# A gated cross- and self-attention block: high parts of queries and keys copied on the chip, and a new order of TensorE's work in the self stage

## The chip, the cores and the metric

The kernel runs on one core of a Trainium2 chip. The metric is the device time of one execution in microseconds (us). Three runs of the kernel before took 2587.09 to 2594.41 us, median 2592.28. All times in timelines are us from the start of the profiled execution's span.

## What is computed

Inputs are x of 32 batches x 100 rows x 512, and a context of 32 x 722 x 512. There are 16 heads of 32. The part that matters here is the second half:

```python
x = x + tanh(g_xattn) * cross_attention(layernorm(x), ctx)
h = layernorm(x)
qkv = (h @ W_qkv).reshape(B, N, 3, 16, 32)
sim = mean over heads of cos(q[:, 5:], q_g)      # scaled to 0..1 over all batches
pos = sim > 0.9
# masked_attn(m): softmax(q k^T / sqrt(32) over the 5 registers and the tokens with m) @ v
x_pos, x_neg = masked_attn(pos), masked_attn(~pos)
reg_out = (x_pos[:, :5] + x_neg[:, :5]) * 0.5
tok_out = where(pos, x_pos[:, 5:], x_neg[:, 5:])
x = x + tanh(g_ffn) * (concat(reg_out, tok_out) @ W_proj + b_proj)
```

All of it is to be exact to about fp32. Fast matmuls take inputs rounded to a short format (fp32r in the listings), so a factor is split into a high and a low part, and a product is three products: high x high, high x low and low x high.

## The kernel before

Four stages follow each other: queries of the cross attention, cross attention, rows (output of the cross attention, layernorm, the q, k and v of the self attention), and the self stage, `stage_self`, from about 2249 us to the end. The rows stage leaves the high and low parts of q and k in DRAM in `qk_parts` (parts 0 to 3: q high, q low, k high, k low), transposed, and values, x1 and the mask tables beside them.

The self stage takes the 32 batches one by one. Its queries and keys come in pairs of batches: `load_pair` fills `q_stack[buf]` and `k_stack[buf]`, each [98, 16 heads, two batches], where rows 0 to 95 are three places of 32 rows each: q high, q low, q high, against k high, k high, k low. One matmul over the 98 rows so gives all three products and, by the last two rows, the mask. A third of either stack is therefore a second copy of a high part, and `load_stacks` (L928) loads it from DRAM as well: for q one load of 64 rows and one of 32, for k one of 32 and one of 64, in pieces of 800 bytes (two batches of one row and head), 1024 pieces for 64 rows and 512 for 32. `load_tables` (L936) adds four small loads of 32 pieces. There are three such buffers (STACKS), so pair p+3 is loaded when pair p has been scored.

All engines run the same loop over batches, written out six batches long (RING), and they meet through semaphores. In `body(b)`, the scores and the softmax of batch b+1, the transposition and mixing of batch b and the projection of batch b-1 stand together:

- SP (queue of loads and stores, in order): store y of b-1 (waits `y_ready`), load x1, wait for `mix_full` of b, load the values of b+3, and in even b load the pair of b+6. Pair 3 follows the mixing of batch 0 in this order, pair 4 that of batch 2.
- PE: `turn_probs(b, n)` transposes a quarter of the probabilities (four heads) into `turned[n % 2]` (L1834), `score(b + 1, j)` makes a quarter of the scores (L1827), `mix(b, n)` multiplies by the values (L1845), `project(b - 1, half)` the output projection (L89 to L91). The order is turn 0, score 0, turn 1, score 1, turn 2, score 2, mix 0, mix 1, project first half, turn 3, score 3, project second half, mix 2, mix 3.
- DVE: `turn_back` n copies a transposed quarter to `pt` (L1750), `shift_of` takes the minimum of the (negated) scores (L1739), `fold_registers` (L1762, L1764), `split_mix` makes `ot_lo` (L1768), `invert` the reciprocals (L1746), `result` makes y (L1775). Order: copy 0, minimum 0, fold, copy 1, split, minimum 1, copy 2, minimum 2, reciprocal 0, copy 3, minimum 3, reciprocal 1, result, reciprocals 2 and 3. There are two y buffers; `result` waits until the store of two batches before has landed.
- ACT: `high_part` makes `ot_hi` of b-1 (L1705), then exponentials 0 to 3 of b+1 (L1713).
- POOL: scales the four quarters of the probabilities (L1679), each after its reciprocal; in even b it then waits for the loads of pair b/2+1 and copies its register columns (L951).

## Time and profile before

| what | value |
|---|---|
| median of three runs | 2592.28 us |
| profiled execution: time, span | 2588.93, 2587.1 us |
| PE busy in the span | 2478.7 us, 96% |
| DVE, ACT, POOL busy | 1804.8, 1332.2, 491.6 us |
| mean granted TensorE clock | 0.971 |
| queue q1 (SP's loads and stores) | 375.71 MB, 61.2% of 16 engines' span |

The self stage is the last 13% of the span. In the page's forty slices it is the last five or so: DMA is at nine tenths there and TensorE's clock at eight or nine tenths. A timeline shows each instruction's start and duration; for SP the duration is that of the issue, not of the transfer. TensorE's matmuls are pipelined, so a duration is longer than the distance to the next start.

### The profile page before, as it was taken

How to read it: one execution, taken by the hardware profiler on the slowest of the kernel's cores; microseconds unless marked ns; L12 is line 12 of the kernel's file. 1: busy time of each engine (PE TensorE's matmuls, PEld its weight loads, DVE VectorE, ACT ScalarE, POOL GpSimd, SP SyncE). 2: the span in 40 equal slices, each digit the busy share in tenths (PEclk: the TensorE clock that was granted, in tenths of full speed). 3: DMA queues.
4: the chain of work that ended last, by engine and by line, in shares of the span. 5: the costliest groups of instructions: out<-in, count | busy, mean ns of one | idle time of the engine just before them, and what ended most of it. 6: DMA issues, size and time to landing. Idle time of an engine off the chain costs nothing. (4 is left out here: it accounts for less than half of the span.)

```text
span 2587.1 us, 47522 instructions
## 1 busy us (share of the span) xinstructions
PE 2478.7 (96%) x17128; PEld 2223.4 (86%) x17128; DVE 1804.8 (70%) x2998; ACT 1332.2 (51%) x3000; POOL 491.6 (19%) x412
## 2 busy tenths in 40 slices
PE   6899999999999999999999999999959999889998
PEld 6889999999999999999999999999858888677776
DVE  7567777777777777777777777777757666565665
ACT  3355555555555545555555555545534444455564
POOL 0311111111111111111111111111024333133333
PEclk9999999999999999999999999999969999889999
DMA  7645554555545555545554455554459999899994
GB/s 223 205 122 131 124 131 120 131 128 131 132 117 128 130 133 128 131 117 130 129 132 122 128 125 129 131 132 126 106 150 192 214 211 198 207 175 189 192 185 105
DMA packets 324312, 379.82 MB, mean 147 GB/s; under 512 B 125814, under 2 KB 231702, under 8 KB 324118
## 3 DMA queue, kind: packets, MB, share of 16 engines
q1 hardware_dynamic: 322414, 375.71, 61.2%
q8 instruction: 132, 2.16, 0.4%
q10 hardware_dynamic: 1704, 1.43, 0.2%
q14 instruction: 62, 0.51, 0.1%
HBM read 162.48 MB, written 72.57 MB: 91 GB/s over the span
## 5 line engine op out<-in xcount | busy, mean ns | idle before, releaser
L740 DVE TENSOR_TENSOR c_parted<-c_prob,c_parted 128x600 fp32r<-128x600 f32 x512 | 400.6, 783 | 363.4 <-ACT c_prob L686 363.4
L864 PE MATMUL c_mix<-c_parted,c_v 120*66 120x200 f32 (+1 forms) x3072 | 544.9, 270 | 0.7 <-DVE c_parted L740 0.6
L849 PEld LDWEIGHTS c_pair<-c_q_stack,c_k_stack 100*120 100x120 f32 (+1 forms) x3072 | 517.7, 186 | 10.7 <-issue 6.1
L849 PE MATMUL c_pair<-c_q_stack,c_k_stack 100*120 100x100 f32 (+1 forms) x3072 | 520.0, 227 | 6.1 <-DVE c_parted L740 4.5
L726 DVE TENSOR_REDUCE c_peak<-c_pair 100x1 f32<-100x724 f32 x512 | 456.9, 908 | 55.2 <-PE c_pair L811 39.7
L682 ACT ACTIVATE c_parted<-c_pair 128x600 fp32r<-128x600 f32 x512 | 344.9, 674 | 283.0 <-PE c_pair L849 282.8
L864 PEld LDWEIGHTS c_mix<-c_parted,c_v 120*66 120x66 f32 (+1 forms) x3072 | 418.3, 140 | 3.1 <-DVE c_parted L740 0.9
L664 ACT ACTIVATE c_v<-c_work 120x512 fp32r<-120x512 f32 (+1 forms) x192 | 115.7, 603 | 442.3 <-PE c_work L91 442.3
L686 ACT ACTIVATE c_prob<-c_pair 128x600 f32<-128x600 f32 x512 | 341.4, 667 | 0.0
L811 PE MATMUL c_pair<-c_k_stack,c_q_stack 96*100 96x362 f32 x1024 | 254.4, 329 | 0.0
L617 POOL TENSOR_TENSOR c_ct_lo<-e_stage,c_ct_hi 128x722 fp32r<-128x722 f32 x64 | 111.8, 1747 | 747.1 <-ACT c_ct_hi L650 747.1
L617 POOL TENSOR_TENSOR f_ct_lo<-e_stage,f_ct_hi 128x722 fp32r<-128x722 f32 x60 | 104.8, 1747 | 718.5 <-ACT f_ct_hi L650 718.5
L811 PEld LDWEIGHTS c_pair<-c_k_stack,c_q_stack 96*100 96x100 f32 x1024 | 169.6, 166 | 60.4
L674 ACT ACTIVATE c_k_hi<-c_work,f_key_bias 128x362 fp32r<-128x362 f32 (+1 forms) x256 | 144.9, 567 | 105.3 <-PE c_work L91 85.7
L720 DVE SCALAR_TENSOR_TENSOR c_k_lo<-c_work,f_key_bias,c_k_hi 128x362 fp32r<-128x362 f32 (+1 forms) x256 | 149.8, 586 | 54.4 <-ACT c_k_hi L674 54.4
L1713 ACT ACTIVATE s_prob<-s_scores,s_shift 106x100 f32<-106x100 f32 x512 | 168.1, 368 | 34.5 <-DVE s_shift L1739 34.5
L89 PE MATMUL c_work<-f_ct_hi,w_wk_hi 128*128 128x362 f32 (+1 forms) x512 | 176.7, 345 | 8.6 <-PEq L153 4.5
L89 PE MATMUL c_work<-c_ct_hi,w_wk_hi 128*128 128x362 f32 (+1 forms) x512 | 175.0, 342 | 0.0
L91 PE MATMUL c_work<-f_ct_hi,w_wk_lo 128*128 128x362 f32 (+1 forms) x512 | 169.4, 331 | 0.0
L90 PE MATMUL c_work<-f_ct_lo,w_wk_hi 128*128 128x362 f32 (+1 forms) x512 | 169.1, 330 | 0.0
L91 PE MATMUL c_work<-c_ct_hi,w_wk_lo 128*128 128x362 f32 (+1 forms) x512 | 167.9, 328 | 0.0
L90 PE MATMUL c_work<-c_ct_lo,w_wk_hi 128*128 128x362 f32 (+1 forms) x512 | 167.9, 328 | 0.0
(205 smaller groups left out, 5292.7 us busy)
## 6 DMA issues: line engine op xcount, KB each, us to landing
c_k_stack<-c_k_hi SPq DMA_DIRECT2D x1024, 90.2 KB, 2.1
e_stage<-in_ctx SPq DMA_DIRECT2D x32, 1444.0 KB, 6.3
c_k_stack<-c_k_lo SPq DMA_DIRECT2D x512, 90.2 KB, 2.1
c_q_stack<-q_parts SPq DMA_DIRECT2D x192, 100.0 KB, 2.4
mix_parts<-w_mixed SPq DMA_DIRECT2D x64, 200.0 KB, 3.2
r_parts<-mix_parts SPq DMA_DIRECT2D x22, 512.0 KB, 7.1
s_q_stack<-qk_parts SPq DMA_DIRECT2D x10, 800.0 KB
s_k_stack<-qk_parts SPq DMA_DIRECT2D x10, 800.0 KB
```

Source lines behind the costliest of these rows:

```text
L89: pe.matmul(out, left_hi, right_hi, start=first, stop=False)
L90: pe.matmul(out, left_hi, right_lo, start=False, stop=False)
L91: return pe.matmul(out, left_lo, right_hi, start=False, stop=last)
L617: pool.tensor_tensor(ct_lo[odd][:, k, :], columns[:, k, :], ct_hi[odd][:, k, :], ALU.subtract).then_inc(ct_lo_done, 1)
L682: act.activation(parted[i % PR][:, :, 0, :].rearrange("p (a t) s -> p a t s", a=2), logits, ACT.Exp).then_inc(exp_hi_done, 1)
L686: act.activation(prob[i % 2][:, :, :].rearrange("p (a t) s -> p a t s", a=2), logits, ACT.Exp).then_inc(exp_done, 1)
L726: dve.tensor_reduce(peak[:, i:i + 1], pair[i % 2][0:S, :, 0:HALF], AX.XY, ALU.max).then_inc(peak_done, 1)
L740: dve.tensor_tensor(p[:, :, 1, :], prob[i % 2][:], p[:, :, 0, :], ALU.subtract).then_inc(p_lo_done, 1)
L811: last = pe.matmul(pair[i % 2][0:S, bank, 0:HALF], q_stack[0:STACK, i, :], k_stack[0:STACK, i, cols], start=True, stop=True)
L849: return pe.matmul(pair[i % 2][0:r, t // (CT // 2), col:col + S], k_stack[:, i, c_cols(t)], q_stack[:, i, :], start=True, stop=True)
L864: return pe.matmul(mix[g % 2][0:VW, at * 2 * S:(at + 1) * 2 * S], v[0:r, t, i, :], parted[i % PR][0:r, t, :, :].rearrange("p a s -> p (a s)"),
L1713: last = act.activation(prob[:, j, k, :], scores[0:QR, j, k * S:(k + 1) * S], ACT.Exp, bias=shift[:, at:at + 1], scale=-1.0, accum_out=tot ...
```

## The change

From pair 3 on, `load_stacks` makes one load for q (places 0 and 1) and one for k (places 1 and 2). The missing third is copied on the chip, in four pieces of four heads: ACT copies q high from place 0 to place 2, DVE copies k high from place 1 to place 0. The pieces of pair p stand in the bodies of batches 2p-4 (pieces 0 and 1) and 2p-3 (2 and 3); the first scores of the pair are made in the body of 2p-1. A piece waits for the pair's loads. In ACT's order a piece stands behind exponentials 1 and another behind exponentials 3; in DVE's order one behind reciprocal 0, ahead of copy 3, and one behind reciprocal 1, ahead of the result. POOL's register copies wait for q's third, the first score of a pair for both. Pairs 0 to 2 are loaded whole, in a changed order of k's two loads.

TensorE's order becomes turn 0, score 0, turn 1, score 1, turn 2, score 2, turn 3, score 3, the whole projection of b-1, then mix 0 to 3. Turn 3 gets a wait for DVE's copy 1, and the wait for `y_ready` stands ahead of the mixing, now behind the projection.

```diff
-A_PAIR_LOADS = 8
+WHOLE_LOADS, PAIR_LOADS = 8, 6
+WHOLE_PAIRS = 3
+
+
+def pair_landed(buf, before):
+
+    return 16 * (PAIR_LOADS * (before + 1) + (WHOLE_LOADS - PAIR_LOADS if buf < WHOLE_PAIRS else 0))
...
-def load_stacks(engine, qk_parts, q_stack, k_stack, first, landed):
-    for stack, at, places in ((q_stack, SIDE, ((0, 0, 2), (2, 0, 1))), (k_stack, 0, ((0, 2, 1), (1, 2, 2)))):
-        for place, part, parts in places:
+def load_stacks(engine, qk_parts, q_stack, k_stack, first, landed, whole=True):
+    for stack, at, places in ((q_stack, SIDE, ((0, 0, 2), (2, 0, 1))), (k_stack, 0, ((1, 2, 2), (0, 2, 1)))):
+        for place, part, parts in places if whole else places[:1]:
             src = qk_parts[part:part + parts].rearrange("a (d h) n -> (a d) h n", h=H)
             engine.dma_start(f32(stack[place * HD:(place + parts) * HD, :, at:at + 2 * S]),
                              src[:, :, bass.ds(first * S, 2 * S)]).then_inc(landed, 16)
...
+        def thirds_in(i, before, more):
+
+            ahead = (i + 4 - i % 2) // 2
+            if not more or (before < RING and ahead < WHOLE_PAIRS):
+                return 0, 0, ()
+            return ahead % STACKS, ahead // STACKS, (2, 3) if i % 2 else (0, 1)
...
                 pool.memset(f32(q_stack[buf][0:STACK, :, at:at + 1]), 0.0).then_inc(cleared, 1)
             pool.wait_ge(cleared, 2 * (STACKS - 1))
 
-            def copies(buf, pairs_before):
-                pool.wait_ge(pair_in[buf], (pairs_before + 1) * 16 * A_PAIR_LOADS)
+            def copies(buf, pairs_before, whole=False):
+                pool.wait_ge(pair_in[buf], pair_landed(buf, pairs_before))
+                if whole is not True:
+                    pool.wait_ge(q_third, HPT * (STACKS * pairs_before + buf - WHOLE_PAIRS + 1))
                 copy_registers(pool, q_stack[buf], unit_column, copies_done)
...
-            def body(b, i, deep, pair, before, last):
+            def copy_third(buf, before, n):
+                act.wait_ge(pair_in[buf], pair_landed(buf, before))
+                heads = slice(n * HPT, (n + 1) * HPT)
+                act.activation(q_stack[buf][2 * HD:3 * HD, heads, SIDE:SIDE + 2 * S],
+                               f32(q_stack[buf][0:HD, heads, SIDE:SIDE + 2 * S]), ACT.Copy).then_inc(q_third, 1)
+
+            def body(b, i, deep, pair, before, last, u, more=True):
                 odd = i % 2
                 if before:
                     high_part(b - 1, 1 - odd)
+                buf, turns, pieces = thirds_in(i, before, more)
+                half = len(pieces) // 2
                 if not last:
-                    for j in range(HPT):
-                        exponentials(b + 1, 1 - odd, j)
+                    exponentials(b + 1, 1 - odd, 0)
+                    exponentials(b + 1, 1 - odd, 1)
+                for n in pieces[:half]:
+                    copy_third(buf, u + turns, n)
+                if not last:
+                    exponentials(b + 1, 1 - odd, 2)
+                    exponentials(b + 1, 1 - odd, 3)
+                for n in pieces[half:]:
+                    copy_third(buf, u + turns, n)
...
-            def body(b, i, deep, pair, before, last):
+            def copy_third(buf, before, n):
+                dve.wait_ge(pair_in[buf], pair_landed(buf, before))
+                heads = slice(n * HPT, (n + 1) * HPT)
+                dve.tensor_copy(k_stack[buf][0:HD, heads, 0:2 * S], f32(k_stack[buf][HD:2 * HD, heads, 0:2 * S])
+                                ).then_inc(k_third, 1)
...
+                buf, turns, pieces = thirds_in(i, before, more)
+                half = len(pieces) // 2
                 turn_back(b, 0)
                 if not last:
                     shift_of(b + 1, 0)
                 if not last:
                     shift_of(b + 1, 2)
                     invert(b + 1, 1 - odd, 0)
+                for n in pieces[:half]:
+                    copy_third(buf, u + turns, n)
                 turn_back(b, 3)
                 if not last:
                     shift_of(b + 1, 3)
                     invert(b + 1, 1 - odd, 1)
+                for n in pieces[half:]:
+                    copy_third(buf, u + turns, n)
                 if before:
...
-            def score(b, i, j, pairs_before):
+            def score(b, i, j, pairs_before, whole=False):
 
                 buf, odd = i // 2, i % 2
                 if not odd and j == 0:
-                    pe.wait_ge(pair_in[buf], (pairs_before + 1) * 16 * A_PAIR_LOADS)
+                    pe.wait_ge(pair_in[buf], pair_landed(buf, pairs_before))
                     pe.wait_ge(copies_done, 2 * STACKS * pairs_before + 2 * buf + 2)
+                    if not whole:
+                        pe.wait_ge(q_third, HPT * (STACKS * pairs_before + buf - WHOLE_PAIRS + 1))
+                        pe.wait_ge(k_third, HPT * (STACKS * pairs_before + buf - WHOLE_PAIRS + 1))
...
                 turn_probs(b, 2)
                 if not last:
                     score(b + 1, at, 2, step)
-                if before > 1:
-                    pe.wait_ge(y_ready, b - 1)
-                mix(b, odd, 0, place, deep)
-                mix(b, odd, 1, place, deep)
+                pe.wait_ge(pt_done, b * HPT + 2)
+                turn_probs(b, 3)
+                if not last:
+                    score(b + 1, at, 3, step)
                 if before == 1:
                     pe.wait_ge(w_split, 2)
                 if before:
                     project(b - 1, 1 - odd, 0)
-                turn_probs(b, 3)
-                if not last:
-                    score(b + 1, at, 3, step)
-                if before:
                     project(b - 1, 1 - odd, 1)
-                mix(b, odd, 2, place, deep)
-                mix(b, odd, 3, place, deep)
+                if before > 1:
+                    pe.wait_ge(y_ready, b - 1)
+                for n in range(HPT):
+                    mix(b, odd, n, place, deep)
```

## Rows read from the trace of the kernel before

**Rows 1.** Busy time in stretches: engine busy us (instructions), granted clock, DMA share, GB/s.

```profile
2380.00:2400.00 20.00, 17.19 (x142) 13.89 (x141) 11.17 (x31) 10.27 (x60) 6.61 (x10) 0.91 0.94 192
...
2552.68:2561.12 8.44, 8.44 (x78) 6.96 (x77) 6.10 (x16) 5.84 (x33) 3.38 (x5) 1.00 0.24 76
```

**Rows 2.** Timeline of SyncE's queue: start, duration of the issue, line.

```profile
2249.64 1.29 SPq L932 DMA_DIRECT2D s_q_stack<-qk_parts  x2
...
2262.71 3.04 SPq L932 DMA_DIRECT2D s_q_stack<-qk_parts  x2
...
2284.54 3.01 SPq L932 DMA_DIRECT2D p_q_stack<-qk_parts  x2
...
2302.60 2.97 SPq L932 DMA_DIRECT2D s_q_stack<-qk_parts  x2
...
2500.50 3.55 SPq L932 DMA_DIRECT2D s_q_stack<-qk_parts  x2
...
2517.76 0.56 SPq L1635 DMA_DIRECT2D out<-s_y  x1
...
2521.76 3.05 SPq L932 DMA_DIRECT2D p_q_stack<-qk_parts  x2
```

**Rows 3.** DMA of one period, from 2362.19 to 2382.22.

```profile
DMA packets 3918, 3.74 MB, mean 186 GB/s; under 512 B 258, under 2 KB 3330, under 8 KB 3916
```

**Rows 4.** Waits from 2303 to 2540: us, times, longest.

```profile
DVE s_y L1775 <- DMA out<-s_y: 38.1, 12, 5.7
```

**Rows 5.** Timeline of TensorE: start, duration, instruction, [idle before <- released by].

```profile
2552.68 0.57 PE L1834 MATMUL s_turned<-e_ident,s_prob 106*100 106x106 f32 x4
...
2554.94 1.31 PE L1845 MATMUL s_out_bank<-s_pt,s_values 100*32 100x106 f32 x16
...
2556.18 0.47 PE L89 MATMUL s_out_bank<-s_w_hi,s_ot_hi 128*100 128x512 f32 x1
```

**Rows 6.** Timeline of DVE in the same batch.

```profile
2554.58 0.59 DVE L1750 COPY s_pt<-s_turned 100x424 f32<-100x424 f32 x1
...
2555.24 0.57 DVE L1768 TENSOR_TENSOR s_ot_lo<-s_out_bank,s_ot_hi 128x400 fp32r<-128x400 f32 x1
...
2557.20 0.17 DVE L1746 RECIPROCAL s_inv<-s_total 106x4 f32<-106x4 f32 x1
```

**Rows 7.** Timeline of POOL, its register copies at the start of the stage.

```profile
2267.07 0.59 POOL L951 TENSOR_TENSOR s_q_stack<-s_q_stack,p_unit_column 96x80 fp32r<-96x80 f32 x2 [8.18 <-DMA s_q_stack<-tables]
...
2290.23 0.61 POOL L951 TENSOR_TENSOR s_q_stack<-s_q_stack,p_unit_column 96x80 fp32r<-96x80 f32 x2 [4.42 <-DMA s_q_stack<-tables]
```

**Rows 8.** Groups by line and shape, whole span: busy us, mean ns | idle before.

```profile
L1679 POOL TENSOR_TENSOR s_prob<-s_prob,s_inv 106x400 f32<-106x400 f32 x128 | 107.8, 854 | 192.7 <-DVE s_inv L1746 192.5
...
L650 ACT ACTIVATE c_ct_hi<-e_stage 128x722 fp32r<-128x722 f32 x64 | 51.0, 796 | 0.0
...
L1440 DVE COPY w_mixed<-w_mixed 32x224 f32<-32x224 f32 x1 | 0.3, 265 | 0.0
...
L1806 DVE TENSOR_TENSOR s_w_lo<-e_stage,s_w_hi 128x2048 fp32r<-128x2048 f32 x1 | 5.3, 5331 | 1.6 <-ACT s_w_hi L1726 1.6
...
L1304 DVE TENSOR_TENSOR r_w_lo<-e_stage,r_w_hi 128x2048 fp32r<-128x2048 f32 x1 | 2.3, 2292 | 0.8 <-ACT r_w_hi L1197 0.8
```

**Rows 9.** Timeline of TensorE, whole self stage.

```profile
2284.38 0.57 PE L1834 MATMUL s_turned<-e_ident,s_prob 106*100 106x106 f32 x4
...
2307.11 0.92 PE L1834 MATMUL s_turned<-e_ident,s_prob 106*100 106x106 f32 x4 [4.25 <-POOL s_prob L1679]
...
2316.55 0.57 PE L1834 MATMUL s_turned<-e_ident,s_prob 106*100 106x106 f32 x4
...
2407.88 2.10 PE L1845 MATMUL s_out_bank<-s_pt,s_values 100*32 100x106 f32 x16 [0.93 <-DMA s_values<-values]
...
2512.36 0.57 PE L1834 MATMUL s_turned<-e_ident,s_prob 106*100 106x106 f32 x4
...
2569.56 0.93 PE L1834 MATMUL s_turned<-e_ident,s_prob 106*100 106x106 f32 x8
```

More of the change, by code:

```diff
@@ L1593, in stage_self @@
         cleared = m.sem("cleared")
+        q_third, k_third = m.sem("q_third"), m.sem("k_third")
         block = ctx.enter_context(nc.Block())
@@ L1600, in all_batches, with load_pair @@
             for i in range(RING):
-                body(i, i, i // DEEP, i // 2, i, False)
+                body(i, i, i // DEEP, i // 2, i, False, 0)
             with engine.Fori(1, TAIL // RING) as u:
                 for i in range(RING):
-                    body(u * RING + i, i, u * (RING // DEEP) + i // DEEP, u * STACKS + i // 2, RING, False)
+                    body(u * RING + i, i, u * (RING // DEEP) + i // DEEP, u * STACKS + i // 2, RING, False, u)
             for b in range(TAIL, B):
-                body(b, b % RING, b // DEEP, b // 2, RING, b == B - 1)
+                body(b, b % RING, b // DEEP, b // 2, RING, b == B - 1, b // RING, (b + 4 - b % 2) // 2 < PAIRS)
+        def thirds_in(i, before, more):
[3 more added lines that the diff above has]
+            return ahead % STACKS, ahead // STACKS, (2, 3) if i % 2 else (0, 1)
         @block.sync
         def _(sp):
-            def load_pair(first, buf):
-                load_stacks(sp, qk_parts, q_stack[buf], k_stack[buf], first, pair_in[buf])
+            def load_pair(first, buf, whole=False):
+                load_stacks(sp, qk_parts, q_stack[buf], k_stack[buf], first, pair_in[buf], whole)
                 load_tables(sp, table_dram, q_stack[buf], k_stack[buf], first, pair_in[buf])
@@ L1622, in _ @@
             sp.wait_ge(cleared, 2 * (STACKS - 1))
-            load_pair(2, 1)
+            load_pair(2, 1, True)
             load_values(1, 1)
@@ L1630, in _ @@
             for n in range(2, STACKS):
-                load_pair(2 * n, n)
+                load_pair(2 * n, n, True)
             def store(b, odd):
@@ L1686, in _ @@
                 if b % 2 == 0:
-                    copies((b + 2) // 2 % STACKS, (b + 2) // RING)
+                    copies((b + 2) // 2 % STACKS, (b + 2) // RING, (b + 2) // 2 < WHOLE_PAIRS)
             with pool.Fori(1, TAIL // RING) as u:
@@ L1697, in _ @@
                 if b % 2 == 0 and b + 2 < B:
-                    copies((b + 2) // 2 % STACKS, (b + 2) // RING)
+                    copies((b + 2) // 2 % STACKS, (b + 2) // RING, (b + 2) // 2 < WHOLE_PAIRS)
         @block.scalar
@@ L1776, in result, with body @@
                                          ).then_inc(y_ready, 1)
-            def body(b, i, deep, pair, before, last):
+            def copy_third(buf, before, n):
[3 more added lines that the diff above has]
+                                ).then_inc(k_third, 1)
+            def body(b, i, deep, pair, before, last, u, more=True):
                 odd = i % 2
+                buf, turns, pieces = thirds_in(i, before, more)
+                half = len(pieces) // 2
                 turn_back(b, 0)
@@ L1865, in body @@
                 if not last:
-                    score(b + 1, at, 0, step + (i + 1) // RING)
+                    score(b + 1, at, 0, step + (i + 1) // RING, before < RING and (i + 1) // 2 < WHOLE_PAIRS)
                 if before:
@@ L1883, in body @@
                     project(b - 1, 1 - odd, 0)
-                turn_probs(b, 3)
-                if not last:
-                    score(b + 1, at, 3, step)
-                if before:
                     project(b - 1, 1 - odd, 1)
-                mix(b, odd, 2, place, deep)
-                mix(b, odd, 3, place, deep)
+                if before > 1:
+                    pe.wait_ge(y_ready, b - 1)
+                for n in range(HPT):
+                    mix(b, odd, n, place, deep)
             for j in range(HPT):
-                score(0, 0, j, 0)
+                score(0, 0, j, 0, True)
             for i in range(RING):
```

## The prediction

> **What bounds the kernel now.** I read the page first: TensorE is busy 96% of the span, so a share of busy time decides nothing, and the change touches only the self stage, the last 340 us. There I read stretches of 20 us, then the stretch of one batch late in the stage, then the queue of SyncE, then each engine's timeline.
>
> Two regimes stand side by side. In the middle of the stage the DMA engines are busy 94%, TensorE only 17.2 of 20 us, and its granted clock is 0.91 in one such stretch [rows 1]. In the batch from 2552.68 to 2561.12, when no pair loads are left, TensorE is busy in all of its 8.44 us at full clock, while DVE has 6.10, ACT 5.84 and POOL 3.38 us of work and DMA is at 0.24 [rows 1]. So a batch costs 8.44 us when TensorE alone sets it.
>
> The middle does not reach that. SP issues the loads of a pair of batches at 2302.60 for the fifth pair and at 2521.76 for the sixteenth and last: 11 periods in 219.2 us, 19.9 us a pair. Of such a period the issue itself takes 17 us (2500.50 to the store at 2517.76) [rows 2], because the queue is full. One period moves 3918 packets [rows 3]; by the code 3072 of them are the 800-byte pieces of queries and keys, some 600 are values, x1 and results, 128 are tables. The stores wait behind the pair's loads in SP's queue, and so the result on DVE waits for a y buffer, 38.1 us in 12 times in this stretch [rows 4]; behind it wait the reciprocals, POOL's scaling and TensorE's transposition. The reader is to see that the bound of the middle is the DMA traffic seen through one in-order queue, with TensorE 1.4 us a batch behind it.
>
> **What the loads cost after the change.** From the fourth pair on, the third load of q (32 partitions) and of k go: 1024 of 3072 packets. Priced from three places: the steady period, 19.9 us for 3800/16 = 237 packets an engine, 84 ns each; the first pair of the stage, issued at 2249.64 and landed when POOL's copies began at 2267.07, 17.4 us [rows 2, 7], at most 17.4/206 = 84 ns (values of one batch with it, and nothing taken off for latency); the second, issued at 2262.71 behind the first and landed by 2290.23, 23.2 us after the first for some 231 packets, 100 ns. So 64 packets fewer an engine are 4.8 to 6.4 us (lower end: pair one with 2 us of latency taken off, 75 ns); I take 84 ns, 5.4 us. The DMA period falls to about 14.5 us, under 2 x 8.44. DMA stops being the rate.
>
> **What the order on TensorE costs.** Work is the same, but two covers go. In the covered batch, counted from its first transposition at 2552.68, three transposition-score pairs take 2.26 us, half of the mixing 1.24 us, then the projection starts at 3.50 [rows 5]. The fourth transposition needs the buffer that copy 1 on DVE frees, done at 2554.58+0.59, so 2.49; the projection needs ot_lo, done at 2555.24+0.57, so 3.13 [rows 6]. Before, mixing lay between, so both were ready. Now the fourth transposition is next at 2.26 and waits until about 2.5, and the projection follows its scores at about 3.25, just after ot_lo. That is 0.3 us of waiting a batch: 8.7 us, 17.4 a pair. In the other direction, scores 3 come 2.7 us earlier, so exponentials 3 have more room.
>
> **What the copies cost.** ACT gets two copies a batch of 32 partitions x 800 elements. Nearest row: a copy in SBUF of 722 elements, 0.80 us [rows 8]; scaled 0.88. 5.84+1.76 = 7.6 us, below 8.7. DVE gets two as well. The nearest row is a copy in SBUF of 224 elements, 0.27 us [rows 8]: between 0.27 (nothing scales) and 0.95 (all scales); I take the middle, 0.6. 6.10+1.2 = 7.3 us, at the upper end 8.0. Neither is the bound by itself. The Trainium skill (VectorE: DVE Perf Modes, "Mode 2x_2P") says an fp32 copy within SBUF runs at two elements a cycle; by its figure for such copies (the section on the TRN2 errata) one would take an estimated 0.48 us and the sum would be the same.
>
> **The added wait.** Both engines now wait for the load itself. DVE's first copy of a pair stands behind reciprocal 0, which is at 2557.20, 4.5 us into the batch [rows 6], so at about 4.7; behind it are queued copy 3 of the probabilities, the minimum of scores 3, the result and the reciprocals 1 to 3. ACT's stands behind exponentials 1 at about 5.1; behind it exponentials 2 and 3. TensorE's transpositions 2 and 3 of the next batch and mixing 3 of this one wait for those. Going through that order, DVE may come 1.2 us late and ACT 1.4 before TensorE is held: DVE by the chain minimum, exponentials 3, reciprocal, scaling.
>
> The load is issued some 0.7 us after the mixing of batch b, an even one, and is wanted in b+2: 8.7+4.7 = 13.4 us after that mixing, harmless until 14.6. When does it land? Pair one with 5.4 us off lands 12.0 us after issue: 12.7. With pair two's 100 ns for 128+8 packets of its own and 19 of store, x1 and values ahead, plus 1 us until the first packet: 16.5, so 17.2. I take the middle, 15.0: 0.4 us late a pair. So 17.8 us a pair (17.4 to 20.0).
>
> POOL's register copies now wait for ACT's thirds, a batch ahead of their use: nothing, as those end within a microsecond of exponentials 3, whose scaling POOL awaits anyway. TensorE's added waits for both are a batch old by then: nothing. SP's stores come out of its queue earlier; nothing waits for that any more.
>
> **The sum**, against the profiled execution (span 2587.1, time 2588.93; the median of the runs is 2592.28, 3.35 above). Start: whole loads of pairs 1 and 2 are as before. Pair 3 is issued at 2284.54 [rows 2] and is now wanted in batch 2, which begins at 2284.38 [rows 9], so at 2289.1, and lands at about 2298: 9 us, less 1.2 of slack, 7.7, and TensorE restarts at a low clock. What that costs is seen in batch 4 before, where after 4.25 us idle a group of transpositions takes 0.92 us rather than 0.57 [rows 9]; the slow stretch there costs about 2.4 us. That stall of batch 4, 6.65 in all, goes. With 0.3 x 3 for the order: +7.7+2.4+0.9-6.65 = +4.4. Middle: from 2316.55 to 2512.36 [rows 9] 10 pairs took 195.8 us, now 178.0: -17.8. End: batches 25 to 30, 57.2 us to 2569.56 [rows 9], now 6 x 8.7: -5.0. The last batch has no scores between its transpositions to cover copy 1 and ot_lo, and loses the cover of mixing for both: an estimated 8.65 us for 7.55, +1.1. Together -17.3 us: 2571.6 for the profiled execution, 2575.0 from the median. I say 2573.
>
> **The rivals.** (a) The load comes late, and the clock makes it dear: slower than before. Price: at 100 ns a packet it lands at 17.2, 2.6 past the slack. The trace shows what idle time of that size does: after 0.93 us without work the mixing of 2407.88 takes 2.10 us where it is 1.31 in a covered batch [rows 5, 9], and with the projection after it some 1.6 us are lost. A pair is then 17.4+2.6+1.6 = 21.6, 2.0 more than now: 10 x 2.0 + 4.4 - 5.0 + 1.1 = +20, so 2612. It is slower from a pair of 19.6, that is, from a landing at about 15.2 if the clock falls with it, or 16.8 if not. Against it: the traffic ahead is lighter than for pair two. (b) DVE and POOL get into each other's way. POOL's scaling starts as soon as reciprocal 0 or 1 ends, exactly when DVE's copies start. The row for it: a subtraction of 2048 elements on DVE takes 2.29 us alone and 5.33 while POOL scales four times [rows 8]. If each copy waits for a scaling of 0.85 us [rows 8], DVE has 7.3+1.7 = 9.0 a batch and its late reciprocals hold transpositions: 9.1 to 9.3 a batch, 18.4 a pair: -11, 2581. The Trainium skill states the rule (SBUF — State Buffer, "Who interferes with whom"): a two-port copy and a GpSimd instruction exclude each other and the first to start keeps the ports; by it, if DVE starts first, POOL waits and nothing is lost. The trace agrees that one is held for long: 5.33 against 2.29 us. (c) The packets are not what fills the queue (a fixed cost a load, the tables), and the period stays near 19.6: the change does not do what it says, within 5 us of before. For it: the issue times show that the queue is full, not what fills it. Against: the stage's DMA share of 0.94 falls to 0.24 as soon as pair loads are over [rows 1]. (d) A pair lands in between, 18.4 to 19.3, near -5 us: the same within what can be told.
>
> **Chances.** Forecast (17.0 to 18.2 a pair) 0.60, 2565 to 2581; (b) 0.11; (a) 0.14; (c) 0.06; (d) 0.09. A measurement of this kernel tells 0.3%, 8 us. Faster: 0.60+0.11 = 0.71; same: 0.15; slower: 0.14. The range from 2563 to 2596 leaves out about 0.06 below and most of (a) above.
>
> **What would show it.** SP's issue of a pair down from 17 to 10 to 12 us with gaps behind it; DMA share of the middle near 0.75; no wait of the result for a store; DVE's and ACT's thirds at 0.6 and 0.9 us; a wait of about 0.25 us before the fourth transposition in each batch; a wait of about 9 us for the load in batch 2, then under 1 us a pair. Wrong if DVE's first third of a pair waits 2 us or more, if the clock in the middle is below 0.95, or if a batch at the end takes over 9 us.

## The result, and the profile after

The changed kernel takes 2585.7 us (median of 11 runs, 2582.55 to 2589.23) against 2592.28 (11 runs of before, 2585.11 to 2596.53): a ratio of 0.9978, 95% interval 0.9970 to 0.9986. That is 5.7 us (the medians lie 6.6 apart), about a third of the forecast of 17.3. The sign was right and the size was not. The time lies in the stated range and near the price of rival (d). The profiled execution has a span of 2585.0 us and a time of 2586.86.

First the stage by stretches. A batch is counted from its first transposition (L1834 before, L1880 after), read from TensorE's timeline; all numbers are us.

| | batch 0 starts | batches 0 to 4 | 5 to 24 (a pair) | 25 to 30 | 31 to the end | span |
|---|---|---|---|---|---|---|
| before | 2255.69 | 60.86 | 195.81 (19.58) | 57.20 | 17.54 | 2587.1 |
| forecast, change | 0 | +4.4 | -17.8 (17.80) | -5.0 | +1.1 | -17.3 |
| after | 2259.03 | 70.43 | 184.87 (18.49) | 54.52 | 16.15 | 2585.0 |
| measured, change | +3.3 | +9.6 | -10.9 | -2.7 | -1.4 | -2.1 |

The later start of batch 0 comes from ahead of the stage, in code that the change doesn't touch (the stage's first load of q and k is issued at 2252.99 for 2249.64), and over the profiles of this study it lies between 2255.7 and 2262.9 us. So single spans are worth less here than the stretches and the ratios of the runs.

The middle first, as in [rows 1]: the same columns, after.

```profile
2380.00:2400.00 20.00, 17.84 (x157) 14.12 (x155) 14.48 (x36) 15.18 (x70) 8.70 (x11) 1.00 0.66 155
...
2544.16:2552.40 8.24, 8.03 (x77) 6.67 (x77) 6.05 (x16) 5.73 (x33) 3.93 (x7) 1.00 0.25 75
```

DMA is no longer the bound: its share is 0.66 where it was 0.94. A covered batch at the end takes 8.24 us; it was 8.44, and the forecast for it was 8.7. Two such batches would be 16.5 us, yet a pair takes 18.49. TensorE is without work 2.16 us in those 20. The waits, from 2330 to 2500, say behind whom (total us, times, longest). The group of [rows 4], the result's wait for a store, is gone, in the stretch of that row too.

```profile
DVE s_k_stack L1812 <- DMA s_q_stack<-tables: 12.7, 6, 2.8
DVE s_inv L1777 <- ACT s_prob L1729: 10.4, 16, 0.9
ACT s_q_stack L1736 <- DMA s_q_stack<-tables: 10.0, 6, 2.3
PE s_turned L1880 <- DVE s_pt L1781: 10.0, 28, 0.4
...
DVE p_k_stack L1812 <- DMA p_q_stack<-tables: 4.7, 3, 2.2
```

Both copying engines wait for the load: of the eleven pairs 5 to 15 DVE does in all, ACT in ten. DVE's first thirds of these pairs wait 2.29, 2.17, 2.69, 1.90, 2.17, 1.09, 1.97, 0.40, 2.78, 1.62 and 2.79 us, 2.0 in the mean. The forecast named 2 us as the sign that it is wrong; six of the eleven are above it.

What it does to TensorE stands in the timelines of DVE and, behind it, of TensorE (start, duration, instruction, [idle before <- released by]):

```profile
2418.71 0.57 DVE L1812 CAST p_k_stack<-p_k_stack 32x800 fp32r<-32x800 f32 x1 [2.17 <-DMA p_q_stack<-tables]
2419.20 0.58 DVE L1781 COPY s_pt<-s_turned 100x424 f32<-100x424 f32 x1
```

```profile
2411.84 0.57 PE L1880 MATMUL s_turned<-e_ident,s_prob 106*100 106x106 f32 x4
...
2414.47 0.56 PE L1880 MATMUL s_turned<-e_ident,s_prob 106*100 106x106 f32 x4 [0.29 <-DVE s_pt L1781]
...
2418.12 2.64 PE L1891 MATMUL s_out_bank<-s_pt,s_values 100*32 100x106 f32 x32
2420.68 0.57 PE L1880 MATMUL s_turned<-e_ident,s_prob 106*100 106x106 f32 x4
...
2421.84 0.57 PE L1880 MATMUL s_turned<-e_ident,s_prob 106*100 106x106 f32 x4 [0.25 <-POOL s_prob L1695]
...
2423.15 0.57 PE L1880 MATMUL s_turned<-e_ident,s_prob 106*100 106x106 f32 x4 [0.42 <-DVE s_pt L1781]
...
2424.44 0.94 PE L1880 MATMUL s_turned<-e_ident,s_prob 106*100 106x106 f32 x4 [0.39 <-DVE s_pt L1781]
...
2426.31 0.63 PE L90 MATMUL s_out_bank<-s_w_lo,s_ot_hi 128*100 128x512 f32 x1
...
2431.69 0.57 PE L1880 MATMUL s_turned<-e_ident,s_prob 106*100 106x106 f32 x4
```

The batch from 2411.84 holds the wait: 8.84 us, and the mixing at 2418.12 is drawn out to 2.64 because copy 3 on DVE stands behind the third. More comes in the next batch as three small idle times of TensorE, 0.25, 0.42 and 0.39 us, where a covered batch has one, of 0.29. Behind the third of them its clock falls from 2.4 to 1.2 GHz: a group of transpositions takes 0.94 us for 0.57, a projection matmul 0.63 for 0.39. That batch takes 11.01 us. Batches 6 to 24 take 9.16, 9.43, 8.84, 9.43, 9.36, 9.44, 9.01, 9.44, 8.84, 11.01, 8.31, 8.88, 9.06, 11.03, 8.32, 8.29, 9.45, 11.01, 8.29: the three of 11.0 are those in which the clock fell. The same three idle times, to 0.01 us, stand in seven of these batches; where the clock holds, such a batch takes 9.4 us.

Now the start. Pair 3's load, and the two engines and TensorE behind it:

```profile
2289.60 1.37 SPq L938 DMA_DIRECT2D p_q_stack<-qk_parts  x1
2291.02 2.11 SPq L938 DMA_DIRECT2D p_k_stack<-qk_parts  x1
2293.17 4.16 SPq L947 DMA_DIRECT2D p_k_stack<-tables  x1
```

```profile
2306.17 0.56 DVE L1812 CAST p_k_stack<-p_k_stack 32x800 fp32r<-32x800 f32 x1 [16.83 <-DMA p_q_stack<-tables]
```

```profile
2307.30 1.62 PE L1891 MATMUL s_out_bank<-s_pt,s_values 100*32 100x106 f32 x8 [14.73 <-DVE s_pt L1781]
```

It is a wait of 16.83 us where 9 were forecast. Pair 3 is issued at 2289.60, 30.6 us after the stage's first transposition (28.9 before), and the first third starts 16.6 us later, where 13.5 was forecast.

Last, the queue itself in the middle. The row to compare with is [rows 2], where a pair's issue took 17 us:

```profile
2386.58 0.58 SPq L938 DMA_DIRECT2D s_q_stack<-qk_parts  x1
2387.35 0.58 SPq L938 DMA_DIRECT2D s_k_stack<-qk_parts  x1
2388.12 2.37 SPq L947 DMA_DIRECT2D s_k_stack<-tables  x1
2390.68 0.95 SPq L949 DMA_DIRECT2D s_q_stack<-tables  x1
2391.82 0.90 SPq L947 DMA_DIRECT2D s_k_stack<-tables  x1
2392.91 0.89 SPq L949 DMA_DIRECT2D s_q_stack<-tables  x1
```

It is over in 7.2 us. Only the first two of these loads are large; the four after them, of 32 small pieces each, take 5.1 of the 7.2 us, and the one that the thirds wait for last is the last table load: it lands by 2400.43, 13.9 us after the first issue. In the last 1.4 us before it the DMA share is 0.37 (2399 to 2400) and then 0.12 (2400 to 2400.43): most of the sixteen engines are idle by then, and the wait is for the tail.

### The profile page after: what moved, and what is told of

Read it like the earlier page. It is cut to its first block and busy times, and to the rows that moved or that the text cites. A ratio compares the mean times of both kernels' runs of the same rounds, so it can differ in the third digit from the quotient of the medians.

```text
span 2585.0 us, 47643 instructions
## 1 busy us (share of the span) xinstructions
PE 2469.3 (96%) x17128; PEld 2216.9 (86%) x17128; DVE 1833.3 (71%) x3050; ACT 1377.7 (53%) x3052; POOL 508.2 (20%) x412
## 3 DMA queue, kind: packets, MB, share of 16 engines
q8 instruction: 132, 2.16, 0.4%
```

## Experiments

Ratios are to the kernel before on the same chip, with 95% intervals. "A pair" is the mean over batches 5 to 24, as in the table above.

**The order alone, and the copies alone.** The first takes the kernel before and gives TensorE only the new order:

```diff
+                pe.wait_ge(pt_done, b * HPT + 2)
+                turn_probs(b, 3)
+                if not last:
+                    score(b + 1, at, 3, step)
...
+                if before:
+                    project(b - 1, 1 - odd, 0)
                     project(b - 1, 1 - odd, 1)
...
+                for n in range(HPT):
+                    mix(b, odd, n, place, deep)
```

> The kernel before with TensorE's new order alone (whole loads, no copies on the chip). Theory A (loads and the wait for them decide): the queue of loads still sets the middle at about 20 us a pair, so within 3 us of before; a covered batch late in the stage takes 8.2 us rather than 8.4, as in the trace of the changed kernel. Theory B (the order itself costs 0.3 us a batch, as the prediction had it): covered batches take 8.7 us and the time is 2 to 4 us above before.

Ratio 1.0000 (0.9986 to 1.0014), a pair 19.51 us for 19.58, batches 25 to 30 56.51 for 57.20. The covered batches at the end take 8.23 to 8.24 us, as in the changed kernel, and 8.44 before: where nothing else holds TensorE, the order saves 0.2 us a batch. The second keeps everything of the change but that order:

```diff
-                pe.wait_ge(pt_done, b * HPT + 2)
-                turn_probs(b, 3)
...
+                mix(b, odd, 0, place, deep)
+                mix(b, odd, 1, place, deep)
...
                     project(b - 1, 1 - odd, 0)
+                turn_probs(b, 3)
```

> The changed kernel with TensorE's old order (thirds copied on the chip kept). Theory A (the engines' wait for the load in the middle of an even batch decides): batch 2 waits for pair 3 as long as in the changed kernel (15 to 17 us on DVE), pairs in the middle take about 18.5 to 19 us, time within 3 us of the changed kernel. Theory B (the new order is what loses the gain): pairs at 17.4 or less and the time 10 us or more below the changed kernel.

Ratio 0.9978 (0.9964 to 0.9991), a pair 18.43, batches 0 to 4 69.24: all of the change's gain, and all of its loss at the start. So the order is neither the gain nor the trouble. In the first its effect can't be seen where the DMA traffic sets the rate (share 0.94 from 2380 to 2400, as before).

**Is it the wait for the load?** Three kernels try to move or remove it. The first moves the thirds of an even batch behind its last reciprocal (DVE) and last exponentials (ACT):

```diff
-                half = len(pieces) // 2
+                half = len(pieces) // 2 if odd else 0
...
+                if not odd:
+                    for n in pieces:
+                        copy_third(buf, u + turns, n)
```

> The changed kernel with both pieces of an even batch moved to its end: on ACT behind exponentials 3, on DVE behind reciprocal 3; odd batches stay. The wait for the load comes 3 to 4 us later in the batch. Theory A (the wait for the load sets the middle): it goes in nearly all pairs, a pair takes 16.5 to 17.2 us rather than 18.5, and batch 2 waits about 4 us less; together 15 to 20 us below the changed kernel. Theory C (the copies' own time and the port that DVE and POOL share set the middle): no change, pairs stay at 18.5.

Ratio 0.9922 (0.9902 to 0.9942), a pair 17.88, the start 65.17: 0.6 us a pair and 5.3 at the start back. I had expected 16.5 to 17.2 a pair. From 2330 to 2500 no engine waits for a load any more, so what is left is the place itself. Two thirds stand in a row ahead of copy 0 of the next batch, which frees the buffer of TensorE's third transposition (DVE, then TensorE):

```profile
2374.13 1.91 DVE L1813 CAST s_k_stack<-s_k_stack 32x800 fp32r<-32x800 f32 x2
2375.97 0.58 DVE L1782 COPY s_pt<-s_turned 100x424 f32<-100x424 f32 x1
```

```profile
2376.68 0.56 PE L1885 MATMUL s_turned<-e_ident,s_prob 106*100 106x106 f32 x4 [0.62 <-DVE s_pt L1782]
```

The second lets the thirds copy from and into scratch buffers with no load behind them; the queue, the loads and the copies' size stay, and the third places of the stacks keep what pairs 0 to 2 left there:

```diff
-                dve.wait_ge(pair_in[buf], pair_landed(buf, before))
-                heads = slice(n * HPT, (n + 1) * HPT)
-                dve.tensor_copy(k_stack[buf][0:HD, heads, 0:2 * S], f32(k_stack[buf][HD:2 * HD, heads, 0:2 * S])
+                dve.tensor_copy(scratch_k[0:HD, n, :, 0:2 * S], f32(scratch_k[HD:2 * HD, n, :, 0:2 * S])
```

> The changed kernel in which ACT and DVE make their copies, of the same shapes and at the same places, between scratch tiles and wait for no load; the third rows of the stacks keep the data of pairs 0 to 2, so its output is not the reference's. It prices the wait alone. Theory A: the whole wait goes: a pair takes 16.5 to 17 us rather than 18.5, batch 2 no longer waits 17 us, and the time is 25 to 30 us below the changed kernel. Theory C (copies and the port that DVE and POOL share): pairs still 18 or more, at most 12 us below, from the start of the stage alone.

Ratio 0.9844 (0.9829 to 0.9859). A pair takes 16.71 us, batches 0 to 4 60.30, batches 25 to 30 49.52. So the wait costs 1.8 us a pair, 10.1 us at the start and 5.0 in batches 25 to 30: 33 us together, with the clock that falls behind it. (The ratios, 0.9978 and 0.9844, lie 35 us apart.) The third leaves the thirds out as well:

```diff
-                dve.wait_ge(pair_in[buf], pair_landed(buf, before))
-                heads = slice(n * HPT, (n + 1) * HPT)
-                dve.tensor_copy(k_stack[buf][0:HD, heads, 0:2 * S], f32(k_stack[buf][HD:2 * HD, heads, 0:2 * S])
-                                ).then_inc(k_third, 1)
+                dve.sem_inc(k_third, 1)
```

> The changed kernel without the copies and without their wait: ACT and DVE only raise the semaphores. The third rows of the stacks keep the data of pairs 0 to 2, so its output is not the reference's. Beside the run that copies between scratch tiles without a wait it prices the copies themselves. Theory C (copies and the port shared by DVE and POOL cost time): pairs take 16.4 or less and the time is 4 us or more below. Theory A: pairs 16.5 to 16.7, the same.

2551.49 us in one run (before, beside it: 2594.6), a pair 16.60. By one profile of either kernel the copies themselves cost 0.1 us a pair at these places. The rival of the shared port, which was to bring a pair to 18.4, falls with this. It would have been easy to take for right, since a pair did come out at 18.49.

**What makes the load late?** If the small table loads come late because they stand behind the large ones, it should help to issue them first. Nothing else is changed:

```diff
             def load_pair(first, buf, whole=False):
 
-                load_stacks(sp, qk_parts, q_stack[buf], k_stack[buf], first, pair_in[buf], whole)
                 load_tables(sp, table_dram, q_stack[buf], k_stack[buf], first, pair_in[buf])
+                load_stacks(sp, qk_parts, q_stack[buf], k_stack[buf], first, pair_in[buf], whole)
```

> The changed kernel with the four small table loads of a pair issued ahead of its two large loads. Theory D (the small loads, issued last behind a full queue, are what lands last): landing after the first issue falls from 13.9 us to 12 or less, pairs to 17.5, and the time by 8 us or more. Theory E (the slowest of the DMA engines has its share of the large loads to finish, whatever stands last): landing within 0.7 us of 13.9 after the first issue, time within 4 us of the changed kernel.

Ratio 0.9876 (0.9860 to 0.9891), a pair 17.07, the start 64.59. SP's queue and, behind it, DVE's thirds in this kernel:

```profile
2394.60 0.25 SPq L947 DMA_DIRECT2D p_k_stack<-tables  x1
2395.03 0.25 SPq L949 DMA_DIRECT2D p_q_stack<-tables  x1
2395.48 0.24 SPq L947 DMA_DIRECT2D p_k_stack<-tables  x1
2395.91 0.24 SPq L949 DMA_DIRECT2D p_q_stack<-tables  x1
2396.34 0.59 SPq L938 DMA_DIRECT2D p_q_stack<-qk_parts  x1
2397.12 0.59 SPq L938 DMA_DIRECT2D p_k_stack<-qk_parts  x1
```

```profile
2407.04 0.56 DVE L1812 CAST p_k_stack<-p_k_stack 32x800 fp32r<-32x800 f32 x1 [0.83 <-DMA p_k_stack<-qk_parts]
```

The same six loads are issued in 3.1 us instead of 7.2, and the last lands 12.4 us after the first issue (13.9 in the changed kernel). The group of waits from 2330 to 2500 shrinks from 12.7 and 4.7 us to this:

```profile
DVE s_k_stack L1812 <- DMA s_k_stack<-qk_parts: 3.9, 5, 1.3
...
DVE p_k_stack L1812 <- DMA p_k_stack<-qk_parts: 2.7, 3, 1.0
```

The same two lines swapped in the kernel before, where the bytes are still all loaded:

> The kernel before with one edit: the four small table loads of a pair are issued ahead of its four large loads. Theory F (the bytes of the loads bound the middle of the kernel before, as the prediction had it): the period stays at 19.6 to 20 us a pair, the time within 4 us. Theory G (SP's queue, held for 5 to 7 us a pair by small loads behind a full queue, bounds it): the period falls to 18 us or less and the time by 15 us or more, without any copy on the chip.

Ratio 0.9965 (0.9953 to 0.9978), a pair 19.05 for 19.58, and a DMA share of 0.83 from 2380 to 2400. Most of the period stays, and with it the waits of the result for a store (22.3 us in 8 times from 2330 to 2500, 23.3 in 8 before). So the removed third was needed for the rate; the order in the queue is worth 0.5 us a pair there and 1.4 after the change.

And with the tables first, once more without the new order on TensorE (the kernel of the copies alone, with the same two lines swapped):

> The changed kernel with tables first and with TensorE's old order. Beside the run with tables first and the new order it prices the order where loads no longer cover it. Theory H (the new order saves the 0.2 us a batch that covered batches show, 8.24 against 8.44): pairs take 17.3 to 17.6 rather than 17.07, 5 to 7 us slower than that run. Theory B (the new order costs): 3 us or more faster.

Ratio 0.9886 (0.9868 to 0.9904), a pair 17.16, against 0.9876 and 17.07 with it. The intervals overlap, and the 5 to 7 us that I expected are not there. The two profiles don't price the order closely: without it most batches take 8.44 us, with it 8.31, but the stretch with it holds one batch of 10.68 in which the clock fell. So it is worth 0.1 us a pair as measured, some 0.3 without that batch.

**All four thirds in the odd batch**, where the load is sure to have landed, two in the middle and two behind the last reciprocal; once with pair 2 copied too (and loaded without its third), once with pair 2 whole as in the change. Both have:

```diff
-            ahead = (i + 4 - i % 2) // 2
-            if not more or (before < RING and ahead < WHOLE_PAIRS):
+            ahead = (i + 3) // 2
+            if i % 2 == 0 or not more or (before < RING and ahead < WHOLE_PAIRS):
                 return 0, 0, ()
-            return ahead % STACKS, ahead // STACKS, (2, 3) if i % 2 else (0, 1)
+            return ahead % STACKS, ahead // STACKS, (0, 1, 2, 3)
```

and the first also:

```diff
-WHOLE_PAIRS = 3
+WHOLE_PAIRS = 2
...
-                load_pair(2 * n, n, True)
+                load_pair(2 * n, n, n < WHOLE_PAIRS)
```

> All four pieces of a pair stand in the odd batch (body of 2p-3), two in the middle and two at its end, so their load has one batch more; and pair 2 is loaded without its thirds as well (whole: pairs 0 and 1). Theory A: no engine waits for a load in the middle, and the start loses most of its wait: the third batch starts 8 us or more earlier than in the kernel with late pieces, the pairs take 17 to 17.8 (ACT has 9.3 us of work in an odd batch and hands some over to the even one), time 2557 to 2566. Theory C (the copies bound the middle): as the kernel with late pieces or slower, 2571 to 2580.

> The same placement in odd batches with pairs 0 to 2 loaded whole, as in the changed kernel. Beside the run with two whole pairs it prices the start alone: theory A (the start is bound by the bytes ahead of pair 3 in the queue) has it 5 us or more slower, since 1024 pieces more stand ahead of pair 3; if the start is set by something else they are within 2 us.

Both are slower than the kernel before: 1.0070 (1.0056 to 1.0084) and 1.0050 (1.0035 to 1.0065), a pair 20.89 and 20.96. What I expected was wrong. The wait for the load is gone, and DVE's timeline (three whole pairs) shows what took its place:

```profile
2407.96 1.71 DVE L1812 CAST s_k_stack<-s_k_stack 32x800 fp32r<-32x800 f32 x2
...
2412.83 0.18 DVE L1777 RECIPROCAL s_inv<-s_total 106x4 f32<-106x4 f32 x1 [1.13 <-ACT s_prob L1729]
2413.04 1.71 DVE L1812 CAST s_k_stack<-s_k_stack 32x800 fp32r<-32x800 f32 x2
2414.67 0.58 DVE L1781 COPY s_pt<-s_turned 100x424 f32<-100x424 f32 x1
```

ACT has two thirds (1.64 us) before its last exponentials, so the last reciprocal is late; DVE has two thirds behind that, and the copy that frees TensorE's buffer comes after them. TensorE then stands still 2.22 us ahead of the transposition of 2415.38 and falls to 1.2 GHz at 2416.67. Each pair is an 8.3 us batch and a 12.4 us one. In the kernel with two whole pairs there is moreover a wait of 10.3 us for pair 2 in batch 1, so its start is worse (68.85 against 62.75), the opposite of what that variant was for.

**The start, and the load earlier.** With the tables first, only pair 3's thirds (those of batch 2) are put at the end of the batch:

```diff
-                half = len(pieces) // 2
+                half = 0 if before == 2 else len(pieces) // 2
...
+                if not half:
+                    for n in pieces:
+                        copy_third(buf, u + turns, n)
```

> The changed kernel with tables first and, in batch 2 alone, the pieces of pair 3 at the end of the batch. Prices the wait of the start by itself. Theory A: from the first transposition of batch 0 to that of batch 5 it falls from 64.6 to 61 or 62 us, the middle stays at 17.1 a pair, and the time is 2558 to 2561, 2 to 4 us below the run with tables first.

Ratio 0.9868 (0.9851 to 0.9885): the start 61.66 for 64.59, a pair 17.04 for 17.07. To this the last kernel adds that SP issues the load of an even batch at the head of its body, as soon as the scores of the next batch have been taken, and no longer behind the store, the values and the mixing:

```diff
+                if odd == 0 and more_pairs:
+                    sp.wait_ge(scored, (b + 2) * HPT)
+                    load_pair(b + RING, i // 2)
                 if before:
                     store(b - 1, 1 - odd)
...
-                if odd == 0 and more_pairs:
-
-                    sp.wait_ge(scored, (b + 2) * HPT)
-                    load_pair(b + RING, i // 2)
```

> The kernel with tables first and pair 3's pieces late, and with the loads of the next pair issued at the head of SP's body of an even batch, as soon as both batches of the old pair are scored, ahead of the store, of x1 and of the values that wait for the end of the mixing. The load starts some 4 to 5 us earlier against the copies. Theory A (the wait for the load is all that is left in the middle): no wait of DVE or ACT for a load there, pairs at 16.7 us as in the run without a wait, 3 to 4 us below the kernel with tables first and pair 3 late, 2554 to 2558. Theory I (what is left is the stores and values behind the load in the queue): new waits for values or for a y buffer, and no gain.

Ratio 0.9851 (0.9835 to 0.9868), 2554.29 us: the best kernel here, 39 us below the runs of before beside it. A pair takes 16.73 us and the start 59.72, with a wait of 6.81 us left for pair 3. Its waits of DVE from 2330 to 2500 hold none for a load; what leads is ACT:

```profile
DVE s_inv L1776 <- ACT s_prob L1728: 17.5, 20, 0.9
```

It reaches, with real data, what the kernel without the wait reached (16.73 against 16.71, start 59.72 against 60.30). So in the middle an earlier landing is all that the change lacked: taking the wait away and making the load early give the same pair. At the start this kernel has pair 3's thirds late as well.

## Why the prediction was right and where it failed

**DMA as the bound of the middle: right.** The third of the bytes goes, DMA share falls to 0.66, and the result's wait for a store is gone. The period with fewer packets (2877 against [rows 3]) is no longer filled by them. With the order alone, nothing is gained. Tables first on the kernel before shows that some of the full queue's cost was not bytes: 0.5 of 19.6 us a pair. Rival (c) holds for that part only. The issue of a pair was forecast at 10 to 12 us and is 7.2, and the DMA share at 0.75.

**The order at 0.3 us a batch: wrong in sign.** The wait before the fourth transposition is there, 0.29 us at 2414.47 for 0.25 forecast. The projection's wait for `ot_lo` is not there, and a covered batch takes 8.24 us, 0.2 less than [rows 1] rather than 0.3 more; the kernel with the order alone shows the same. I had added waits to the old sum without asking what ceases with the old order. What in the old order took the 0.2 us is not shown. The error also set the batch at 8.7 for the deadline below.

**The size of the copies: right.** DVE 0.565 us for 0.6, ACT 0.874 for 0.88. Where no load is waited for they are hidden almost wholly: 0.1 us a pair. The Trainium skill (VectorE: DVE Perf Modes, "Mode 2×_2P") has a copy of this kind at two elements a cycle, and by its figures I had estimated 0.48 us; the measured 0.565 is nearer to that estimate than to the 0.95 of a copy all of whose time scales.

**The landing: right in the middle.** 13.1 to 14.7 us after issue in pairs 5 to 15, 13.9 in the mean, for 14.3 taken.

**The deadline and the room behind it: the step that failed.** I had DVE reach its first third 12.7 us after the issue, and let DVE come 1.2 us and ACT 1.4 us late before TensorE is held. That made 0.4 us a pair. Both terms are wrong.

*The deadline.* DVE is at its first third 11.9 us after the issue in the mean (11.95 in the pair issued at 2386.58), and the load lands after 13.9, so it waits 2.0 us. Without the wait the distance is 11.6 to 12.4 from pair 7 on: the batches are 8.3 us long, not 8.7, and the load is issued some 1.1 us after the end of the mixing, not 0.7. In the changed kernel the issue slips further, to 1.9 to 3.0 us in pairs 6 to 15. SP stores y of b-1 ahead of the load, and DVE makes this y behind its second third. At 2381.97 the first third had waited 2.69 us; the result ends at 2385.11, and then:

```profile
2385.14 0.31 SPq L1649 DMA_DIRECT2D out<-s_y  x1
```

x1, the values and, at 2386.58, the load follow. A wait for one load so delays the next load. The kernel that issues the load at the head of the body, ahead of that store, has no such wait.

*The room.* The pair of 2418.71 would take 8.84 + 9.4 us at a full clock, where two batches of the kernel without the wait take 16.6. So of a wait of 2.17 us on DVE and 1.72 on ACT about 1.7 reaches TensorE. The rows give three paths. Mixing 3 waits for copy 3, which stands right behind DVE's third: 0.5 us (2.64 for 2.11). In the next batch the second transposition comes 0.4 us later after the first than in a covered batch, for the scaling behind reciprocal 1, which stands behind copy 3 and minimum 3. And the third transposition waits for copy 0 (ACT, then DVE):

```profile
2418.71 0.87 ACT L1736 ACTIVATE p_q_stack<-p_q_stack 32x800 fp32r<-32x800 f32 x1 [1.72 <-DMA p_q_stack<-tables]
```

```profile
2422.36 0.18 DVE L1777 RECIPROCAL s_inv<-s_total 106x4 f32<-106x4 f32 x1 [0.43 <-ACT s_prob L1729]
2422.45 0.57 DVE L1781 COPY s_pt<-s_turned 100x424 f32<-100x424 f32 x1
```

This path has the least room. ACT's third delays exponentials 2 and 3, reciprocal 3 waits for those, and copy 0 of the next batch stands right behind reciprocal 3 in DVE's order. From ACT's third to the transposition of 2423.15 it is 4.44 us. In the kernel without the wait, where that transposition is not held, it is 4.59 (ACT, then TensorE):

```profile
2411.94 0.87 ACT L1738 ACTIVATE s_scratch_q<-s_scratch_q 32x800 fp32r<-32x800 f32 x1
```

```profile
2416.53 0.55 PE L1882 MATMUL s_turned<-e_ident,s_prob 106*100 106x106 f32 x4
```

So ACT may come some 0.15 us late, not 1.4. I had followed the exponentials only to the reciprocal and the scaling that need them, and not to the copy that merely stands behind that reciprocal. No run moves the thirds of one engine alone, so that ACT's path decides is read from these rows and not tested. The kernel with late thirds and the two with all four in the odd batch have the same tight place: what stands ahead of copy 0 on DVE holds the third transposition.

*The clock.* In three of the pairs from 2330 to 2500 it fell on top of this: 1.6 us each (11.0 for 9.4), 0.5 us a pair over batches 5 to 24. The removal of the wait priced all of it together at 1.8 us a pair; the sum had 0.4. Rival (a) had the mechanism, load late and clock lower, at a landing that didn't come; what made it true in part was the nearer deadline and the missing room. With its price a pair it would have been 21.6; that of rival (d), 18.4 to 19.3 with the load in between, is what happened in the middle.

**The start: mechanism right, size wrong.** +9.6 for +4.4. Pair 3 was put at 13.5 us after its issue, between my bounds of 12.0 and 16.5 (their middle, which I took for the other pairs, is 14.3), and took the upper end of them: the table loads of pair 2 just ahead of it take up to 2.00 us of issue each (at 2282.48), so the queue was still full with whole loads. It is issued 1.7 us later against the stage's start too, by the rows above. Removing the wait gave 10.1 us back, the tables first 5.8, and with them moving only pair 3's thirds another 2.9.

**The end: half of it.** Batches 25 to 30 gave 2.7 for 5.0: the last pairs still have to be waited for, and without the wait they gave 7.7. The last batch was forecast 1.1 us longer and is 0.1 longer up to the end of its mixing (7.76 for 7.62). But the stretch is 1.4 shorter, because the last projection now runs at 2.4 GHz:

```profile
2578.25 0.47 PE L89 MATMUL s_out_bank<-s_w_hi,s_ot_hi 128*100 128x512 f32 x1 [1.64 <-DVE s_ot_lo L1799]
2578.56 0.39 PE L90 MATMUL s_out_bank<-s_w_lo,s_ot_hi 128*100 128x512 f32 x1
```

In the kernel before, the same matmuls took 0.63 us after the same idle time of 1.64. The kernel before with nothing but its tables first has 16.01 in that stretch, and the one with tables first and pair 3 late 17.78, so this is not a gain of the change to count on.

**The balance.** The forecast missed by 15.2 us of span: the middle 6.9, the start 5.2, batches 25 to 30 2.3, batch 0's own place 3.3, less 2.5 in the last. In the middle, a pair without the wait was put 0.7 us too dear (17.4 for 16.7) and the wait 1.4 too cheap (0.4 for 1.8). Two errors of opposite sign covered part of each other, so it is in part luck that the forecast is no further off and its sign right.

## What to carry to other kernels

Where an edit makes engines wait for a load in the middle of their work, the room behind the wait must be followed along every path: through the data, and through whatever merely stands behind a late instruction in its engine's order, into the next batch. It must be done with the batch time that the change itself gives, since a faster loop brings the deadline nearer. And ask whether the wait delays something, here a store, that stands ahead of the next load in its queue. Small loads that gate the use of a buffer belong before the large ones in the same queue; here it was worth 1.4 us a pair. And when a kernel has just left the DMA bound, look once more at where the load is issued, since its old place was chosen by a bound that is gone.

## What the runs showed that I had not expected

- In the middle of the stage a load of 32 small pieces holds its issuing queue for 0.24 us when it stands first. Behind two loads of 1024 pieces it holds it for 0.9 to 3.8 us (4.2 at the start of the stage), and lands after them.
- TensorE's clock fell behind idle times of 0.25, 0.42 and 0.39 us in one batch, in three of the seven batches that have them; behind one idle time of 1.64 us before the last projection it was low in the kernel before and full in the changed one. Idle time alone doesn't tell it, and what else does is open.
- DVE and POOL. In the middle of a batch DVE's third starts first and POOL's scaling takes 1.23 us for 0.85; DVE's copy keeps its 0.57. Two thirds in a row take 1.05 us with POOL idle (2293.02, two whole pairs). They take 1.71 where POOL's scaling comes up during the first (2407.96, three whole pairs): POOL waits for the first third, and the second third waits for POOL. The Trainium skill (SBUF — State Buffer, "Who interferes with whom") says that whoever issues first keeps the shared port and the other blocks; the trace agrees in both cases. Two POOL rows of the changed kernel show the first:

```profile
2398.60 0.86 POOL L1695 TENSOR_TENSOR s_prob<-s_prob,s_inv 106x400 f32<-106x400 f32 x1 [3.03 <-DVE s_inv L1777]
2402.27 1.23 POOL L1695 TENSOR_TENSOR s_prob<-s_prob,s_inv 106x400 f32<-106x400 f32 x1 [2.81 <-DVE s_inv L1777]
```

At 2398.60 DVE was idle, waiting for the load; at 2402.22 its third began 0.05 us before POOL.
